# Mixing and router stage of an adaptive mixture-of-experts block: block-diagonal products replaced by packed 32x32 products, router product in four column groups

## What is computed

```
h    = gelu(gelu(cond @ W0 + b0) @ W1 + b1)
att  = softmax(h @ W2 + b2)                         # (64, 8)
aggw = einsum('bk,koi->boi', att, weight)           # a 32x32 matrix for each sample
xt   = einsum('boi,bih->boh', aggw, x) + (att @ bias_k)[:, :, None]   # mixing
logits = xt @ router_w + router_b                   # (2048, 16)
scores = softmax(logits) + router_bias
gate = top 2 of 16 experts, out of the best 2 of 4 groups
y    = sum over experts of gate * ((silu(xt@w1+b1) * (xt@w2+b2)) @ w3 + b3)
z    = (silu(xt@sw1+sb1) * (xt@sw2+sb2)) @ sw3 + sb3                  # shared expert
out  = x + y + z
```

## Time and profile before

| | |
|---|---|
| median of 3 runs | 261.05 us (260.25 to 266.6) |
| the profiled execution's own time | 260.74 us |
| its span, first to last instruction | 258.8 us |
| mean granted PE clock | 0.993 |
| mixing stage (DVE's first product at 10.57 to PE's first shared product at 58.08) | 47.5 us |
| shared products and dispatch, to the loop's first product | 58.1 to 101.8 us |

### The profile page before, as it was taken

One profiled execution on the slowest core, in us unless ns is written; L12 is line 12 of the kernel. 1 busy time (PEld: TensorE's weight loads), 2 busy tenths in 40 slices (PEclk: granted clock), 3 DMA queues, 4 the chain that ended last, 5 costly groups with the idle time before them and its releaser, 6 DMA issues.

```text
span 258.8 us, 3960 instructions
## 1 busy us (share of the span) xinstructions
PE 241.7 (93%) x1092; PEld 163.9 (63%) x1093; DVE 148.6 (57%) x314; ACT 78.7 (30%) x169; POOL 111.2 (43%) x135
## 2 busy tenths in 40 slices
PE   7947989899999988999999999999999999999975
PEld 6815667688886445677777777777777744444331
DVE  0599698838979978333333444443333311297993
ACT  2223345421227300233333333333433331111300
POOL 7782355421011156365666666666655331000450
PEclk9999799999999999999999999999999999999999
DMA  7998397689154947964545544455555221999954
GB/s 233 339 410 314 147 298 264 236 291 393 39 215 150 417 173 199 371 209 161 163 167 170 176 123 152 131 175 174 174 166 162 82 87 65 397 387 387 400 189 162
DMA packets 20698, 57.90 MB, mean 224 GB/s; under 512 B 2533, under 2 KB 2533, under 8 KB 20428
## 3 DMA queue, kind: packets, MB, share of 16 engines
q1 hardware_dynamic: 15084, 39.89, 42.0%
q0 software_dynamic: 5600, 17.83, 21.4%
HBM read 40.94 MB, written 17.30 MB: 225 GB/s over the span
## 4 chain that ended last, share of the span: by engine, by line
PE 80%; DVE 15%; issue 2%; DMA 1%; ACT 0%; DVEq 0%
PE psum L537 71%; PE psum L683 6%; DVE r L936 3%; DVE xT L1166 3%; DVE xT L931 2%; DVE xT L905 2%; PE psum L580 2%; DVE xT L946 2%; PE psum L696 2%; DMA xT<-cond_pack 1%; DVE x_early L905 1%; DVE mix_bias L933 1%; DVE r L1122 0%; DVE code_f L1100 0%; DVE late_region L905 0%
## 5 line engine op out<-in xcount | busy, mean ns | idle before, releaser
L537 PE MATMUL psum<-wexp,r 128*128 x272 | 68.4, 381 | 0.4 <-DVE r L1122 0.3
L537 PEld LDWEIGHTS psum<-wexp,r 128*128 128x128 f32 x272 | 48.5, 190 | 22.8 <-issue 16.9
L905 DVE TENSOR_TENSOR r<-psum,ebias 128x256 f32<-128x256 f32 x34 | 14.4, 424 | 65.0 <-PE psum L537 65.0
L486 POOL DMA_INDIRECT expert_rows<-late_region,to_row x33 | 33.3, 1010 | 33.0 <-ACT late_region L848 32.7
L476 POOL DMA_INDIRECT late_region<-xt_rows,from_row x36 | 35.3, 981 | 17.9 <-issue 9.7
L537 PE MATMUL psum<-wexp,xt_sb 128*128 x68 | 34.8, 594 | 0.0
L842 ACT ACTIVATE r<-r 128x128 f32<-128x128 f32 x34 | 10.5, 309 | 57.6 <-DVE r L905 57.6
L537 PE MATMUL psum<-xT,shared_sb 128*128 128x512 f32 x64 | 28.0, 593 | 0.0
L848 ACT ACTIVATE late_region<-psum 128x512 f32<-128x512 f32 x34 | 20.3, 598 | 13.9 <-PE psum L537 13.9
L1122 DVE COPY r<-psum 128x512 f32<-128x512 f32 x36 | 24.5, 680 | 0.0
L683 PE MATMUL psum<-ident,late_region 128*128 128x128 f32 x144 | 21.6, 273 | 1.0 <-DMA late_region<-xt_rows,from_row 1.0
(11 more groups left out here) (175 smaller groups left out, 310.2 us busy)
## 6 DMA issues: line engine op xcount, KB each, us to landing
wexp<-expert_pack SPq DMA_DIRECT2D x16, 768.0 KB, 4.7
wexp<-expert_rows SPq DMA_DIRECT2D x8, 1024.0 KB, 12.9
xt_rows<-xt_sb SPq DMA_DIRECT2D x16, 256.0 KB, 2.2
x_early<-x SPq DMA_DIRECT2D x2, 1024.0 KB, 7.6
late_region<-x SPq DMA_DIRECT2D x2, 1024.0 KB, 12.5
ebias<-expert_bias SPq DMA_DIRECT2D x1, 2048.0 KB, 7.8
out_dram<-x_early SPq DMA_DIRECT2D x8, 256.0 KB, 10.0
shared_sb<-shared_pack SPq DMA_DIRECT2D x1, 1536.0 KB, 16.3
```

The lines of the kernel that those rows point to most:

```text
L486: nc.gpsimd.indirect_dma_start(out=y_dram[:, :], out_offset=bass.IndirectOffsetOnAxis(ap=rows.bitcast(U32), axis=0), in_=y_sb[:, slot, :], ...
L537: return nc.tensor.matmul(dst, lhsT, rhs, start=start, stop=stop)
L905: return nc.vector.tensor_tensor(dst, a, b, op)
```

## The change

It does these things.

- **Mixing on PE.** `mix(g)` takes a whole group at once. x is loaded so that partition group i (32 partitions) holds the four samples of tile 4g + i side by side, instead of one below the other. Tile i's four products (K = 32, M = 32, N = 512, float32) read partitions 32i to 32i + 31 and write partitions 32s to 32s + 31 of the tile's bank: 16 products in one group, each at its own place of the array.
- **Mixing on DVE.** `mix(g)` builds 4 x 4 matrices with two instructions, the sum now over adjacent elements; nothing is put on a diagonal and `r1` isn't zeroed. All biases come from two more instructions after a second spreading product, since samples stand in another order in x than in the mixed tiles.
- **Router.** The stationary data are now the router's weights (padded to 32 columns), the moving data the transposed x of a group (512 columns); chunk c writes column group c. ACT copies the four partial results out, and four products a group with a selection matrix `take_expert` add them and turn them back; DVE adds the bias for each group (`group_logits`).
- **Copies.** Of each group's four transposed tiles DVE copies three and ACT one. The ring of mixed tiles has 8 slots, 4 of them in `r1`.
- **Order.** PE issues mix(0), mix(1), then for each group the transposes, with the router's products and sums of the group before and mix(g + 1) between them. The splitting starts with the shared weights; the last 4 of its 12 pieces come behind the stage.
- **DMAs.** x comes in 16 DMAs of 256 KB, 8 issued by SP and 8 by ACT ahead of its first activation. As `x_early` now has another order of rows, the first two groups of x are loaded again (2 MB) behind the stores. DVE waits for the last store of slot 7 before it computes the softmax, as its small results share that memory. The descriptor scratch of POOL's DMAs goes from its default to 4096 bytes.

The diff, cut to its core:

```diff
+    XR = 8
+    EP = 32
...
-        xt_ring = xt_sb[:, :].rearrange("p (r d) -> p r d", d=DIM)
+        xt_ring = [a[:, r * DIM:(r + 1) * DIM] for a in (xt_sb, r1) for r in range(XR // 2)]
...
+        def bank_of(t):
+
+            return t % (2 * GT)
...
+            u = (n + EARLY * GT) % SPLITS if n < SPLITS - EARLY * GT else n - (SPLITS - EARLY * GT)
...
+        def load_mixed(engine, g, row_groups):
+
+            for i in row_groups:
+                rows = x_rows[g * GN + i * P:g * GN + (i + 1) * P, :].rearrange("(s c) d -> c s d", c=IN_C)
+                x_tiles = x_early if g < EARLY else x_late
+                first = g * GT if g < EARLY else (g - EARLY) * GT
+                engine.dma_start(x_tiles[i * IN_C:(i + 1) * IN_C, first:first + GT, :], rows
+                                 ).then_inc(x_loaded[g], 16)
 
...
-                dst = x_early[:, g * GT:(g + 1) * GT, :] if g < EARLY else \
-                    x_late[:, (g - EARLY) * GT:(g - EARLY + 1) * GT, :]
-                sp.dma_start(dst, group_of_x(g)).then_inc(x_loaded[g], 16)
+                load_mixed(sp, g, (0, 1))
...
                 sp.wait_ge(xt_ready, t + 1)
-                sp.dma_start(xt_dram[t * P:(t + 1) * P, :], xt_ring[:, t % RING, :]
-                             ).then_inc(xt_stored[t % RING], 16)
+                sp.dma_start(xt_dram[t * P:(t + 1) * P, :], xt_ring[t % XR]).then_inc(xt_stored[t % XR], 16)
...
+            sp.dma_start(x_early[:, :, :], x_rows[0:EARLY * GN, :].rearrange("(t p) d -> p t d", p=P)
+                         ).then_inc(x_early_loaded, 16)
...
+               att_spread.rearrange("b t k -> b (t k)"))
+            pe.wait_ge(dve_cond, 3)
+            mm(psum[:, 7, NT * KMIX:2 * NT * KMIX], is_block_out.rearrange("b r i -> b (r i)"),
+               att_spread_out.rearrange("b t k -> b (t k)")).then_inc(pe_cond, 1)
...
-            for s in range(NT + 2):
-                if s < NT:
-                    if s % GT == 0:
-                        pe.wait_ge(x_loaded[s // GT], 16)
-                    pe.wait_ge(mix_copied, mixes_until(s))
-                    if s >= 2:
-                        pe.wait_ge(xt_ready, s - 1)
-                    mm(psum[:, s % 2, :], mixT[:, s, :], x_tile(s)).then_inc(xt_done, 1)
...
-                    for c in range(C):
-                        last = mm(psum[:, 4, t * E:(t + 1) * E], xT_tile(t, c), rw_sb[:, c, :],
-                                  start=(c == 0), stop=(c == C - 1))
-            last.then_inc(logits_done, 1)
+            def mix(g):
+
+                pe.wait_ge(x_loaded[g], 16 * BPT)
+                pe.wait_ge(mix_ready, g + 1)
+                x_tiles, first = (x_early, g * GT) if g < EARLY else (x_late, (g - EARLY) * GT)
+                for i in range(GT):
+                    rows = slice(i * IN_C, (i + 1) * IN_C)
+                    for s in range(BPT):
+                        last = mm(psum[s * IN_C:(s + 1) * IN_C, bank_of(g * GT + i), :],
+                                  mixed_w[rows, g * GT + s, :], x_tiles[rows, first + s, :])
+                    last.then_inc(xt_done, 1)
+
+            def transposed(t):
+                if t == 0:
+                    pe.wait_ge(ident_ready, 1)
+                pe.wait_ge(xt_ready, t + 1)
+                for c in range(C):
+                    last = nc.tensor.transpose(psum[:, bank_of(t), c * P:(c + 1) * P],
+                                               xt_ring[t % XR][:, c * P:(c + 1) * P], ident[:, :])
+                last.then_inc(xtT_done, 1)
+
+            def router_products(g):
+
+                if g == 0:
+                    pe.wait_ge(router_loaded, 16)
+                pe.wait_ge(xT_ready, (GT - 1) * (g + 1))
+                pe.wait_ge(xT_act_ready, g + 1)
+                for c in range(C):
+                    last = mm(psum[c * EP:(c + 1) * EP, bank_of(g * GT), :], rw_sb[:, c, :], xT[:, g, c, :])
+                last.then_inc(logitsT_done, 1)
...
+            def router_sums(g):
+
+                pe.wait_ge(logitsT_ready, g + 1)
+                if g == 0:
+                    pe.wait_ge(masks_ready, 2)
+                for u in range(GT):
+                    last = mm(psum[:, bank_of(g * GT + 1), u * E:(u + 1) * E],
+                              logitsT[:, g % 2, u * P:(u + 1) * P], take_expert[:, :])
+                last.then_inc(logits_done, 1)
+
+            mix(0)
+            mix(1)
+            for g in range(NG):
+                for u in range(GT):
+                    transposed(g * GT + u)
+                    if u == 0 and g > 0:
+                        router_products(g - 1)
+                    if u == 2 and g > 0:
+                        router_sums(g - 1)
+                        if g + 1 < NG:
+                            pe.wait_ge(logits_ready, g)
+                            mix(g + 1)
+            router_products(NG - 1)
+            router_sums(NG - 1)
...
-            pe.wait_ge(shared_loaded, 16)
-            pe.wait_ge(split_ready, SPLITS)
+            pe.wait_ge(logits_ready, NG)
+            pe.wait_ge(split_ready, SPLITS - GT)
             shared_up(0, 0)
             shared_up(0, 1)
+            pe.wait_ge(split_ready, SPLITS)
...
+            for g in range(NG):
+                load_mixed(act, g, (2, 3))
...
-            for t in range(NT):
-                act.wait_ge(mix_copied, mixes_until(t))
+            def mixed(t):
+                if t == 0:
+                    act.wait_ge(bias_ready, 1)
                 act.wait_ge(xt_done, t + 1)
-                if t >= RING:
-                    act.wait_ge(xt_stored[t % RING], 16 * (t // RING))
-                    act.wait_ge(xtT_done, t - RING + 1)
-                nc.scalar.activation(xt_ring[:, t % RING, :], psum[:, t % 2, :], ACT.Identity,
+                if t >= XR:
+                    act.wait_ge(xt_stored[t % XR], 16 * (t // XR))
+                    act.wait_ge(xtT_done, t - XR + 1)
+                nc.scalar.activation(xt_ring[t % XR], psum[:, bank_of(t), :], ACT.Identity,
                                      bias=mix_bias[:, t:t + 1]).then_inc(xt_ready, 1)
 
-                if 2 <= t < 2 + SPLITS:
-                    u = t - 2
-                    if u < EARLY * GT:
-                        act.wait_ge(xT_ready, u + 1)
-                    else:
-                        act.wait_ge(shared_loaded, 16)
-                    whole, part, _ = split_of(u)
-                    nc.scalar.activation(part, whole, ACT.Copy).then_inc(part_ready, 1)
+            def transposed(t):
+                act.wait_ge(xtT_done, t + 1)
+                if t // GT == NG - 2:
+                    act.wait_ge(mix_ready, NG)
+                nc.scalar.activation(xT[:, t // GT, :, (t % GT) * P:(t % GT + 1) * P],
+                                     psum[:, bank_of(t), :].rearrange("p (c n) -> p c n", c=C), ACT.Copy
+                                     ).then_inc(xT_act_ready, 1)
+
+            def logits_transposed(g):
+                act.wait_ge(logitsT_done, g + 1)
+                nc.scalar.activation(logitsT[:, g % 2, :], psum[:, bank_of(g * GT), :], ACT.Copy
+                                     ).then_inc(logitsT_ready, 1)
...
+            SPLIT_BEHIND = {5: (0,), 7: (1,), 9: (2,), 10: (3,), 11: (4,), 13: (5,), 14: (6,), 15: (7,)}
+            for g in range(NG):
+                for u in range(GT):
+                    t = g * GT + u
+                    mixed(t)
+                    if u == 0 and g > 0:
+                        transposed(t - 1)
+                    if u == 2 and g > 0:
+                        logits_transposed(g - 1)
+                    for n in SPLIT_BEHIND.get(t, ()):
+                        split(n)
+            transposed(NT - 1)
+            logits_transposed(NG - 1)
+            for n in range(SPLITS - GT, SPLITS):
+                split(n)
...
-            for r in range(RING):
-                act.wait_ge(xt_stored[r], 16 * (NT // RING))
+            for r in range(XR // 2):
+                act.wait_ge(xt_stored[r], 16 * (NT // XR))
...
+            dve.wait_ge(masks_ready, 1)
+            dve.wait_ge(ident_ready, 1)
+            V.tensor_reduce(is_tile_out.rearrange("b (g i) -> b g i", g=NG),
+                            is_place.rearrange("b (i g) j -> b g i j", g=NG), AX_X, ALU.max)
+            link(V.tensor_reduce(is_column, is_place.rearrange("b m j -> b j m"), AX_X, ALU.max))
+            V.tensor_copy(is_block_out, is_column.unsqueeze(2).to_broadcast([BS, BPT, IN_C]))
+            V.tensor_reduce(take_expert[:, :], ident[:, :].rearrange("p (c e) -> p e c", c=C)[:, 0:E, :], AX_X,
+                            ALU.max).then_inc(masks_ready, 1)
...
+            V.scalar_tensor_tensor(out=att_spread_out, in0=att_e.unsqueeze(1).to_broadcast([BS, NT, KMIX]),
+                                   scalar=att_rec, in1=is_tile_out.unsqueeze(2).to_broadcast([BS, NT, KMIX]),
+                                   op0=ALU.mult, op1=ALU.mult).then_inc(dve_cond, 1)
...
```

(64 more changed lines are left out.)

108 lines of the change are left out of this document (56 added, 52 removed).

## The result

The changed kernel takes 254.75 us (median of 4 runs, 252.62 to 256.43) where the kernel before takes 261.22 (4 runs beside it): ratio 0.9747, 95% interval 0.9693 to 0.980, faster by 2.5%. The forecast was 250.0, in a range of 245 to 274.5. Some executions of each kernel have a lower granted clock and take 1.5% or more longer than its fastest (266.6 here, and 256.43); they count in the medians and ranges and are left out of the ratios. The profiled execution of the changed kernel is the one of 256.43 us, with a span of 254.7. A second profile of the same kernel (255.58 us, span 253.8) shows the same picture: there the stage ends at 44.41 and the loop's first product stands at 90.58. Only the first dip of the clock is shorter in it, and the second mixing isn't hit by it (1.15 us).

The account below looks back on a forecast made before the run. PE and DVE were taken as both nearly full and waiting for each other in the stage, then PE alone. The stage ending 10.7 us earlier, everything behind it counted 0, took 260.74 to 250.0 us; range 245 to 274.5.

Parts of the forecast that it names:

- The main choice: PE's mixing: a group's 16 products overlap fully, bounded by issuing 32 pairs, 1.9 us a group; chance 0.50.
- Rival A: PE's mixing: records start strictly in order, only pairs overlap, 7.3 us a group, 273.7 us in all; chance 0.25.
- B: PE's mixing: only four products overlap, 3.4 us a group, 257.1 us in all; chance 0.12.
- D: PE's mixing and router: products don't overlap at all, mixing 13.8 us a group, 307 us in all; chance 0.03.
- a group's matrices: DVE's two mixing instructions: 2.5 us a group, bounds 2.4 to 3.4, depending on whether the stride costs.
- Router and sums: PE, per group: router 1.1 us plus 0.3 for each change between packed and whole array, sums 1.0.
- Period: Stage, from the start of one group's mixing to the next: 7.4 us.
- Set-up: Ahead of the first mixing: ACT's eight DMA issues cost 0.3 us, bounds 0 and 2.0; DVE starts mixing at 11.6.
- Stage's end: PE's first shared product: at 47.4 us, 10.7 earlier, with 1.0 added for hand-overs between engines.
- DVE's wait for the store: Ahead of DVE's softmax: the last store of slot 7 lands at 46 us and costs nothing.
- the slack: DVE's routing behind the stage: `chosen` ends 3.4 us before PE takes it up, which hides small delays.
- What follows the stage: Everything behind the stage: costs nothing more, and the loop's first product stays as far behind as before.

Follow-up runs that it names:

- SP alone: The changed kernel with all 16 loads of x issued by SP and none by ACT: 262.68 us.
- the code moved: The changed kernel with 23 small unused products in PE's set-up, so PE's later instructions stand 92 places further on: 248.75 us.
- in place: The changed kernel with the same 23 small products issued by two short loops, so PE's later instructions move only a few places: 258.14 us.
- the candidate: The changed kernel with DVE's small results moved to att_sb and 23 identity products in PE's first two groups: 248.31 us.
- the old router: The changed kernel with the router's products as before, four per tile with 16 columns: 271.05 us; with added identity products in PE's stops, 274.72 us.

## Why the prediction was right, and where not

The forecast has the direction, the likeliest case and the range right, and its gain is too large: 6.5 us between the medians for 11. The range is wide, as it had to hold a rival by which the kernel would be 5% slower, so the time inside it says little by itself; the rows say more.

- **The main choice** (full overlap, 1.9 us a group): right in kind, and the time was less, 1.15. The 1.9 held 32 pairs at the 0.047 us of the dispatch, whose pairs carry full weights; here issue is no bound at all, as the first 16 records start within 0.11 us. Rival A (7.3), B (3.4) and D (13.8) are out. The second 16 records start 0.45 behind the first: the two records of one product follow each other at their place, those of others don't wait. An estimate by the factor of 10.6 in the Trainium skill ("TensorE: Matmul & The Clock Gate", Part 3: Packing small matmuls) is 1.3, close to the 1.15 seen. The Trainium skill's rule that loads overlap only in other row groups doesn't describe these rows: all 32 loads start within 0.1 us, those of one row group beside running products of the same. The strict order in which products start by the same section would hold for the first records only; 16 second records start behind the first record of the last product.
- **DVE**: a group's matrices 2.44 us (1.22 and 1.22; forecast 2.5). The stride was what had cost.
- **Router and sums**: 1.06 and 1.06 (forecast 1.1 + 0.3 and 1.0). No change of mode was to be seen; 0.3 too much.
- **Period** 5.97 for a forecast of 7.4: 0.75 from the mixing, 0.3 from the router (where 8 pairs at 47 ns and two records would by the way have made 1.24 and not 1.1), the rest waits for copies that I had put at 0.3 each and that stood beside PE's work.
- **Set-up**: this step failed. I let 0.3 us of ACT's eight issues through and DVE start at 11.6; it started at 12.96 (timeline of the changed kernel):

```profile
5.54 0.69 PE L559 MATMUL psum<-xT 128*128 128x64 f32 x2 [1.88 <-DMA xT<-cond_pack]
...
12.96 0.42 DVE L1018 COPY att_sb<-psum 128x256 f32<-128x256 f32 x1 [1.51 <-PE psum L559]
```

  I had priced the issues and not the transfers: `cond_pack` now shares the DMA engines with ACT's queue and lands 1.8 us later (1.3 in the second profile, with the attention at 12.30). The first Gelu started at 6.53 for 4.54, but its delay by ACT's issues was covered, as I had said. With SP alone the attention was there at 11.82, near the forecast. The Trainium skill ("DMA: Bandwidth & Descriptors", Queues, rings and completion order) says that an engine takes turns between the queues that have work; the landings agree with it, 2.9 and 3.3 us with nothing on ACT's queue and 3.9 to 4.7 with two or eight loads there.
- **Stage's end**: 45.44 for 47.4, the sum of a start 1.4 later, a half clock of about 1.0, two periods 1.4 shorter each, and a closing chain of 3.9 for 5.5; the 1.0 that I had added to it for the hand-overs was not needed.
- **DVE's wait for the store**, counted 0: this step failed, and cost 2.3 us in the changed kernel and 2.5 with the code moved. I had let the store land at 46; it landed at 49.6, for a stage that ended 2 us sooner. And the slack that was to hide the rest is 1.4 us and not 3.4, as DVE has more to do between `chosen` and the counts (its idle time of 1.42 in the row of the kernel before, above). Moving the small results frees DVE, but then its products meet POOL's last pieces, which I had counted as free too.
- **What follows the stage**: this step failed most. "The loop's first product as far behind as before" and everything behind it unchanged was the tacit term, and it carried 8.5 us of error, the 2.3 of the store among them. I priced PE's time by records at full clock. Half clock took 3.4 behind the loop; the stop at the loop's end took 2.5. With the code moved, all else equal, the kernel takes 248.75, and the forecast of 250.0 would have been close; part of that is luck: the stage gave 2.2 us more than forecast and the wait for DVE near the end 1.0, which I don't explain, while the way to the loop took 2.5 more.

Where the expected gain went is so shown for the stop (gone with the code moved, back with it in place) and, by the chain, for the store. For the half-clock stretches only their place and price are shown: the ones right behind the stop and near 242 stand in four and in three of the profiles with a stop and in none of the seven without, and the one near 45 came and went between kernels with the same stops of PE around it (0.78, 0.71 and 0.32 us in the changed kernel, the code-moved one and the candidate). How the stage's own 12.6 us divide between the mixing, DVE's shorter work and the router isn't shown either: no run takes the mixing alone back, and the old router came with another clock.
